# Results kept by lower and higher expert, with the last expert's second layer in another layout

## The reference

```python
S = Bb * Tt; C = int(CAP_FACTOR * S / E)                # 320 slots for each of 8 experts
probs = jax.nn.softmax(xf @ gate_w + gate_b, axis=1)
topk_p, topk_i = jax.lax.top_k(probs, TOP_K)            # two experts a token
topk_pn = topk_p / jnp.sum(topk_p, axis=1, keepdims=True)
...
xin = x_pad[idx]                                        # the rows of each expert's slots
h = jax.nn.relu(jnp.einsum('ecd,edh->ech', xin, w1) + b1[:, None, :])
out = jnp.einsum('ech,ehd->ecd', h, w2) + b2[:, None, :]
out = out * jnp.where(valid, tok_w, 0.0)[:, :, None]
final = jnp.zeros((S + 1, d), xf.dtype).at[idx.reshape(-1)].add(out.reshape(-1, d))[:S]
...
x = _layernorm(x + final, axis=-1)
```

## Time and profile before

| | us |
|---|---|
| runs, median (lowest to highest) | 478.04 (474.75 to 478.34) |
| profiled execution, its own time | 475.74 |
| its span, first to last instruction | 473.9 |
| busy: TensorE / VectorE / ScalarE / GpSimd | 402.7 / 363.5 / 243.4 / 145.9 |
| mean granted TensorE clock | 0.921 of full speed |

### The profile page before, as it was taken

The page is one execution under the profiler, slowest core; times in us unless marked ns, Lnnn a source line. Parts: engine busy times, 40 slices in busy tenths (PEclk is TensorE's granted clock), DMA queues, the critical chain, the costliest instruction groups (busy, mean ns, idle before and its releaser), DMA issues.

```text
span 473.9 us, 13604 instructions
## 1 busy us (share of the span) xinstructions
PE 402.7 (85%) x4701; PEld 306.7 (65%) x4701; DVE 363.5 (77%) x1553; ACT 243.4 (51%) x789; POOL 145.9 (31%) x240
## 2 busy tenths in 40 slices
PE   7999999999999999999997761699999999996000
PEld 4556776887888888888885661356776777674000
DVE  5678998888888888888886358867977898793284
ACT  1452666334343343443433253539888988861053
POOL 0056354223031120312203010241354345323384
PEclk9999999999999999999997685599999999999555
DMA  8769400201102011110200001064466545000582
GB/s 278 226 205 409 164 1 3 69 3 34 55 23 66 0 40 48 33 55 0 78 4 24 1 3 45 18 216 129 113 228 205 181 136 178 29 30 28 184 275 97
DMA packets 38238, 46.36 MB, mean 98 GB/s; under 512 B 4155, under 2 KB 32702, under 8 KB 38202
## 3 DMA queue, kind: packets, MB, share of 16 engines
q1 hardware_dynamic: 34474, 35.80, 23.4%
q0 software_dynamic: 3200, 9.40, 5.9%
q10 hardware_dynamic: 528, 0.69, 0.5%
HBM read 34.91 MB, written 11.01 MB: 97 GB/s over the span
## 4 chain that ended last, share of the span: by engine, by line
PE 60%; DVE 14%; ACT 8%; issue 8%; DMA 4%; POOL 3%; SPq 0%; ACTq 0%; POOLq 0%; DVEq 0%
PE bank L876 59%; ACT arena L788 3%; DMA wbuf<-in_w 2%; ACT arena L779 2%; DMA wbuf<-ybuf 1%; DVE kp L1743 1%; DVE vp L1723 1%; DMA bz<-in_b_rows 1%; ACT arena L818 1%; POOL rs L606 1%; PE bank L1252 1%; DVE ub L1331 1%; ACT kp L788 1%; DVE h L1342 1%; DVE mb L1333 1%
## 5 line engine op out<-in xcount | busy, mean ns | idle before, releaser
L623 ACT ACTIVATE rzb<-bank 128x32 f32<-128x32 f32 x128 | 25.4, 199 | 93.3 <-PE bank L876 93.2
L876 PE MATMUL bank<-h,whp 128*128 128x32 f16 x1143 | 59.2, 183 | 0.4 <-DVE h L1345 0.4
L876 PE MATMUL bank<-arena 128*128 128x320 f16 x384 | 54.6, 299 | 0.5 <-DVE arena L1770 0.5
L876 PE MATMUL bank<-arena,kp 128*128 128x320 f16 x384 | 54.5, 299 | 0.0
L1331 DVE TENSOR_TENSOR_SCAN ub<-rzb,bank 128x32 f32<-128x32 f32 x128 | 27.8, 218 | 28.9 <-ACT rzb L623 26.8
L626 ACT ACTIVATE nb<-ub 128x16 f32<-128x16 f32 x128 | 27.9, 218 | 42.2 <-DVE ub L1331 42.2
L876 PEld LDWEIGHTS bank<-arena 128*128 128x128 f16 x384 | 37.2, 99 | 15.0 <-DVE arena L1770 1.0
L876 PEld LDWEIGHTS bank<-arena,kp 128*128 128x128 f16 x384 | 37.3, 98 | 14.1
L876 PEld LDWEIGHTS bank<-h,whp 128*128 128x128 f16 x1143 | 40.8, 96 | 8.3 <-DVE h L1345 0.6
L876 PEld LDWEIGHTS bank<-hsb,at_w 66*64 66x64 f32 x256 | 25.1, 135 | 27.1 <-DVE hsb L1337 14.6
L577 POOL DMA_INDIRECT ybuf<-arena,six x24 | 24.1, 1006 | 59.3 <-DVE arena L1785 54.5
(11 more groups left out here) (214 smaller groups left out, 947.1 us busy)
## 6 DMA issues: line engine op xcount, KB each, us to landing
wbuf<-in_w SPq DMA_DIRECT2D x16, 1024.0 KB
ybuf<-zero POOLq DMA_DIRECT2D x8, 512.0 KB, 7.7
wbuf<-ybuf SPq DMA_DIRECT2D x16, 256.0 KB, 5.9
xin_t<-in_xT SPq DMA_DIRECT2D x16, 128.0 KB, 2.3
arena<-in_ctxT SPq DMA_DIRECT2D x4, 512.0 KB, 7.6
xfin_t<-in_xT SPq DMA_DIRECT2D x16, 128.0 KB, 2.2
xres<-in_xtok SPq DMA_DIRECT2D x16, 128.0 KB, 2.1
x_d<-x SPq DMA_DIRECT2D x8, 256.0 KB, 2.4
```

What stands on the lines that cost most here:

```text
L623: nc.scalar.activation(od(rzb[:]), RZ[j][:, s * 2 * B:(s + 1) * 2 * B], ACT.Sigmoid).then_inc(q["r_ready"], 1)
L876: return nc.tensor.matmul(out_, lhsT, rhs, start=start, stop=stop, skip_group_check=True)
```

## The change

Each token's two experts are sorted by number. The lower expert's result goes to row t of `ybuf`, the higher one's to row 2048 + t. `topf` gets the minimum and the maximum of the two numbers, and the weights `wt` are swapped to match, by twelve small operations that now stand behind expert 7's hidden layer on VectorE. The lower expert is never expert 7, so the lower half of `ybuf` is complete when expert 6 has been scattered. It is loaded as a whole (`ylow`, four DMAs of 512 KB, to the half of `wbuf` that expert 6's weights held) and added to x2 by VectorE, 16 operations. The higher half (`yhigh`, eight DMAs of 256 KB) follows when expert 7's rows have landed. The multiplications by ScalarE (line 857) and the additions by GpSimd (line 599) are gone.

To have expert 6 scattered early, its transposes move from the second layer of expert 7 to behind the third slice of its first layer, and its copies with them. The copies of expert 5 move ahead of the last two weight splits for expert 7.

The second layer of expert 7 is computed with the slots as rows (`rows_out`): the hidden rows are the stationary operand, the weights move, 3 blocks x 8 slices x 3 products = 72 matmuls of 256 columns. VectorE scales them and adds a row of bias (`b2r`, one more small load) and writes `yt` directly; each block is scattered as it becomes ready.

The semaphores `ctx_load0` to `ctx_load3` are renamed `quarter0` to `quarter3` and count the low loads too. Allocations, the further arguments and declarations are left out here.

```diff
+        ylow, yhigh = (view(wbuf, j * TILES * D, TILES, D) for j in range(2))
...
+            sp.dma_start(b2r[:], b2_last.to_broadcast([P, D])).then_inc(q["b2_row"], 16)
...
+            y_v = ybuf.rearrange("(j k p) d -> p j k d", j=2, p=P)
+            sp.wait_ge(q["w_lo"], 4 * (E - 1))
             for j in range(2):
-                sp.wait_ge(q[f"yst{j}"], 16 * CT * (E // 2))
-            y_v = ybuf.rearrange("(j k p) d -> p j k d", j=2, p=P)
+                sp.wait_ge(q[f"yst{j}"], 16 * CT * (E // 2 - j))
+            for i in range(4):
+                sp.dma_start(ylow[:, 4 * i:4 * i + 4, :], y_v[:, 0, 4 * i:4 * i + 4, :]).then_inc(q[f"quarter{i}"], 16)
+            sp.wait_ge(q["w_lo"], 4 * E)
+            sp.wait_ge(q["yst1"], 16 * CT * (E // 2))
             for c in range(CHUNKS):
-                for j in range(2):
-                    sp.dma_start(yg[c][:, 2 * j:2 * j + 2, :], y_v[:, j, 2 * c:2 * c + 2, :]).then_inc(q[f"yl{c}"], 16)
+                sp.dma_start(yhigh[:, 2 * c:2 * c + 2, :], y_v[:, 1, 2 * c:2 * c + 2, :]).then_inc(q[f"yl{c}"], 16)
...
-            scatter(E - 1)
-
-
-            def first_choice(c):
-                pool.wait_ge(q["c_w"], c + 1)
-                if c >= 2:
-                    pool.wait_ge(q["c_b"], 2 * c - 3)
-                pool.tensor_tensor(ca[2 * c % 4], yg[c][:, 0, :], x2[:, 2 * c, :], ALU.add).then_inc(q["c_even"], 1)
+
+            for c, m, col in slots(E - 1):
+                pool.wait_ge(q["yt_ready"], 2 * (E - 1) + c + 1)
+                pool.indirect_dma_start(
+                    ybuf[:, :], bass.IndirectOffsetOnAxis(ap=six[0:m, col], axis=0), yt[1][0:m, c, :], None,
...
-            first_choice(0)
             for c in range(CHUNKS):
-                if c + 1 < CHUNKS:
-                    first_choice(c + 1)
                 rstd_3(c)
 
...
+                if last:
+                    return
...
-            def weighted(c):
-                act.wait_ge(q[f"yl{c}"], 32)
-                nc.scalar.activation(yg[c][:, 0, :], yg[c][:, 0, :], ACT.Copy, scale=wt[:, 0, 2 * c:2 * c + 1]).then_inc(q["c_w"], 1)
-
-            weighted(0)
-            weighted(1)
             for c in range(CHUNKS):
-                if c + 2 < CHUNKS:
-                    weighted(c + 2)
                 act.wait_ge(q["rstd3"], c + 1)
...
+            def rows_out(e, j):
+
+                for c in range(CT):
+                    m = min(P, CAP - c * P)
+                    if c == 2:
+                        pe.wait_ge(q["yt_ready"], 2 * e)
+                    for f in range(FK):
+                        if c == 0:
+                            pe.wait_ge(q["h_lo"], FK * e + f + 1)
+                            if f % 4 == 0:
+                                pe.wait_ge(q["w_lo"], 4 * e + f // 4 + 3)
+                        for n, (a, b) in enumerate(PAIRS):
+                            last = mm(bank[(6, 7, 0)[c]][0:m, 0:D], hp[b][:, f, c * P:c * P + m], w2p[j][a][:, f, :],
+                                      f == n == 0, f == FK - 1 and n == 2)
+                    last.then_inc(q["last_mm"], 1)
+
...
+                    if f == 2 and last_:
+                        pe.wait_ge(q["yT_ready"], 2 * e)
+                        pe.wait_ge(q["yt_ready"], 2 * e - 2)
...
+                if last_:
+                    return rows_out(e, j)
...
                     if f == 3 and not first:
-                        if not last_:
-                            pe.wait_ge(q["xlo_ready"], 2 * e + 4)
-                        else:
-                            pe.wait_ge(q["yt_ready"], 2 * e - 2)
+                        pe.wait_ge(q["xlo_ready"], 2 * e + 4)
...
-            pe.wait_ge(q["yt_ready"], 2 * E - 2)
-            results_T(E - 1)
...
-            then(nc.vector.tensor_copy(topf[:], topi[:, :, 0:2]))
+            nc.vector.tensor_tensor(topf[:, :, 0], topi[:, :, 0], topi[:, :, 1], ALU.min)
+            then(nc.vector.tensor_tensor(topf[:, :, 1], topi[:, :, 0], topi[:, :, 1], ALU.max))
...
-            nc.vector.tensor_tensor(wsum[:], top[:, :, 0], top[:, :, 1], ALU.add).then_inc(q["ws_ready"], 1)
-            dve.wait_ge(q["ws_ready"], 1)
-            nc.vector.reciprocal(wsum[:], wsum[:]).then_inc(q["ws_ready"], 1)
-            dve.wait_ge(q["ws_ready"], 2)
-            for j in range(2):
-                nc.vector.tensor_tensor(wt[:, j, :], top[:, :, j], wsum[:], ALU.mult)
...
+                    if f == 2 and last:
+                        results(e - 1, 1 - j, 16 * CT * i)
...
-                    if p == 3 and not (isinstance(e, int) and e == 0):
+                    if p == (1 if isinstance(e, int) and e == E - 2 else 3) and not (last or isinstance(e, int) and e == 0):
...
-            results(E - 1, 1, 16 * CT * (E // 2 - 1))
-
+
+            ws = [0]
+
+            def weigh(ins):
+                ws[0] += 1
+                ins.then_inc(q["ws_ready"], 1)
+                dve.wait_ge(q["ws_ready"], ws[0])
+
+            nc.vector.tensor_tensor(turned[:], topi[:, :, 0], topi[:, :, 1], ALU.is_gt)
+            weigh(nc.vector.tensor_tensor(wsum[:], top[:, :, 0], top[:, :, 1], ALU.add))
+            nc.vector.tensor_scalar(kept[:], turned[:], -1.0, 1.0, ALU.mult, ALU.add)
+            weigh(nc.vector.reciprocal(wsum[:], wsum[:]))
+            for j in range(2):
+                nc.vector.tensor_tensor(wa[:, j, :], top[:, :, j], kept[:], ALU.mult)
+                last = nc.vector.tensor_tensor(wb[:, j, :], top[:, :, 1 - j], turned[:], ALU.mult)
+            weigh(last)
+            for j in range(2):
+                last = nc.vector.tensor_tensor(wa[:, j, :], wa[:, j, :], wb[:, j, :], ALU.add)
+            weigh(last)
+            for j in range(2):
+                last = nc.vector.tensor_tensor(wt[:, j, :], wa[:, j, :], wsum[:], ALU.mult)
+            weigh(last)
+
+            dve.wait_ge(q["b2_row"], 16)
+            dve.wait_ge(q["yst1"], 16 * CT * (E // 2 - 1))
+            for c in range(CT):
+                m = min(P, CAP - c * P)
+                dve.wait_ge(q["last_mm"], c + 1)
+                nc.vector.scalar_tensor_tensor(yt[1][0:m, c, :], bank[(6, 7, 0)[c]][0:m, 0:D], wund[1][0:m, 0:1], b2r[0:m, :],
+                                               ALU.mult, ALU.add).then_inc(q["yt_ready"], 1)
+
+
+            for k in range(TILES):
+                if k % 4 == 0:
+                    dve.wait_ge(q[f"quarter{k // 4}"], 16 + 16)
+                nc.vector.scalar_tensor_tensor(x2[:, k, :], ylow[:, k, :], wt[:, 0, k:k + 1], x2[:, k, :], ALU.mult, ALU.add).then_inc(q["c_low"], 1)
 
             for c in range(CHUNKS):
-                dve.wait_ge(q[f"yl{c}"], 32)
-                k = 2 * c + 1
-                nc.vector.scalar_tensor_tensor(ca[k % 4], yg[c][:, 1, :], wt[:, 0, k:k + 1], x2[:, k, :], ALU.mult, ALU.add).then_inc(q["c_odd"], 1)
+                dve.wait_ge(q[f"yl{c}"], 16)
+                dve.wait_ge(q["c_low"], 2 * c + 2)
+                if c >= 2:
+                    dve.wait_ge(q["o_ready"], c - 1)
                 for i in range(2):
                     k = 2 * c + i
-                    dve.wait_ge(q["c_odd" if i else "c_even"], c + 1)
-                    if c >= 2:
-                        dve.wait_ge(q["o_ready"], c - 1)
-                    nc.vector.scalar_tensor_tensor(cb[k % 4], yg[c][:, 2 + i, :], wt[:, 1, k:k + 1], ca[k % 4], ALU.mult, ALU.add).then_inc(q["c_b"], 1)
+                    nc.vector.scalar_tensor_tensor(cb[k % 4], yhigh[:, k, :], wt[:, 1, k:k + 1], x2[:, k, :], ALU.mult, ALU.add).then_inc(q["c_b"], 1)
                 for i in range(2):
                     k = 2 * c + i
                     dve.wait_ge(q["c_b"], k + 1)
```

22 lines of the change are left out of this document (14 added, 8 removed).

## The result

The changed kernel took 473.52 us in the median of 20 runs (471.34 to 477.25), the kernel before 475.82 beside it (20 runs, 473.57 to 478.42). The ratio is 0.9959, with a 95% interval from 0.9939 to 0.9979: about 1.9 us faster, where the prediction said 7.6. By its own bound of 1% that is no change. The sign held, and so did the stated range of 466 to 475; the size was forecast four times too large. That the range held is in part luck: it was laid around 470 from a median of 478.04 for the kernel before, and in these 20 runs that kernel took 475.82. From that level the forecast would have been 468.2.

The account below looks back on a forecast made before the run. The prediction took serial latency, engines waiting for one transfer or neighbour, as the bound at the end. Its terms, +0.1 - 5.2 - 2.5 = -7.6 us, gave 468.1 from the profiled execution, 470.4 on the median's level; it gave 470, range 466 to 475.

Parts of the forecast that it names:

- They bring nothing: Before expert 0: four small weight operations leaving VectorE's queue gain nothing, since TensorE multiplies filler until 312.12.
- a cost elsewhere: Anywhere else in the kernel: a cost that cancels the gain; chance 0.04.
- The landing of the last scatter: End of expert 7: SP issues the first high load 2.20 us after the last scatter's start, at 438.4.
- Rival 1: End of expert 7: low loads still flow, the last scatter lands 2 us later; -5.6, 472.4 us; chance 0.10.
- the 5.2 forecast: Start of the final chunks' sums after expert 7: at 442.0 instead of 447.19, -5.2 us.
- The ring: Final eight chunks of sums and norm: a pair takes 4.75 us (4.58 to 4.89), 20.5 for 22.98 in all, -2.5.
- Routing: Routing stage near 291 us: one cast becomes min and max, +0.1 us (bounds 0 and 0.2).
- Expert 5's results: Before expert 7: copies of 1.1 us move ahead of VectorE's last two weight splits; nothing is lost.
- Rival 2: Expert 7's second layer: columns don't count, 0.136 us a matmul; -5.7, 472.3 us; chance 0.10.
- Rival 4: Low loads: rows just written load slowly, at 100 GB/s +5.0, 483.0 us; chance 0.04.
- Rival 5: Final chunks: the pace stays 4.89 us a pair and only the start moves; -7.1; within the forecast's 0.64.
- Rival 3: End of expert 7: VectorE's sixteen adds lock out the last scatter's descriptors; -2.2, 475.8 us; chance 0.08.

Follow-up runs that it names:

- after_again: The changed kernel once more, unedited, for a second profile, timed beside the kernel before: 473.6 us, ratio 0.9969.
- the old layout: The changed kernel with the last expert's second layer, transposes, copies and three scatters as before the change: 481.53 us, ratio 1.0115.

## Why the prediction was off

**The step that failed: "They bring nothing: the tensor engine multiplies filler until 312.12".** It asked what the removed operations free, not what they hold back. Without them VectorE's first split starts 0.88 us after the first gather (306.02 and 305.14), where it was 1.59 (306.23 and 304.64), and this shift puts the second and third gather under the splits. TensorE then waits for rows, and in all profiles of this stretch but the first it multiplies at half its clock for a few us behind the wait. The cost is 1.4 us in the first profile (116.02 for 114.65) and 2.6 to 3.1 in the seven others; it is 3.1 in the ratios. The prediction had even named the sign of such a case ("the forecast is wrong if the stretch before 415 us changes by more than the 0.1") and gave a cost elsewhere only 0.04.

**The landing of the last scatter: "SP 2.20 after the last scatter's start".** It measured 3.94, and 4.63 in after_again. The 2.20 was read where no load was in flight. Rival 1 is this step, and its price (2 us later) was about right: 1.7 and 2.4. The prediction's own numbers held the collision: it had the low loads in by 438.0 to 440.7 and the last scatter start at 436.2 (435.4 + 0.77), so "in by 440.7 at the latest" was no argument against it. The data then needed 2.69 for 3.41, which gave 0.7 back. Two smaller terms went the same way. A matmul of 256 columns took 8.14 / 72 = 0.113 for 0.109, 0.29 us in all. The low loads went out at T + 11.43 for T + 10.6, so nearer to the last scatter: 0.6 of that because the scatters of expert 6 stand 1.66 and 1.52 apart instead of 1.28 (the first two end 0.86 and 0.85 us after the end of a split of hidden rows on VectorE), 0.2 because the last of them landed in 2.42. The ring started at T + 23.24 and 23.96 for T + 22.17: 1.1 to 1.8 us of the 5.2 forecast.

**The ring: "a pair takes 4.58 to 4.89, I take 4.75".** It took 5.01, outside the bounds: 1.83 of VectorE, 1.97 to ScalarE, 1.09, 0.12 back. The 1.88 taken as the disturbed step had one of GpSimd's operations beside an add (0.38 in the earlier trace rows); now the next chunk's adds come 0.16 us after the variance and meet two of them, 0.34 and 0.44 for 0.19 each. Cost: 0.86 us over the ring (21.36 for 20.5).

Together, with the usual 2.6 to 3.1 for the first step: -7.6 + (2.6 to 3.1) + (1.1 to 1.8) + 0.9 = -3.0 to -1.8, and -1.9 was measured (-2.9 to -1.0). With the old weight operations kept the first step is gone, and -7.6 + (1.1 to 1.8) + 0.9 = -5.6 to -4.9 stands against a measured -5.1.

**What was right.** Routing cost 0.1 (two operations at 291.49 and 291.60). Expert 6's rows were ready at T + 5.06, as worked out (T + 5.1). VectorE finished expert 7's last block at 437.00 = T + 15.84 for T + 15.6; the twelve weight operations took 1.7 us for 2.2 and delayed no block but the first. Sixteen adds took 6.40 (0.40 each). From ScalarE's end to the span's end it stayed 3.74. "Expert 5's results: nothing is lost" is right in its sum, as the run with them put back shows, though a scatter grew by 1.5 us.

**The rivals.** Rival 1 happened. Rival 2 (columns don't count) fell: 0.113, not 0.136. Rival 4 fell: the low half flowed at 352 GB/s. Rival 5, a ring that stays at 4.89, was too mild: it took 5.01 (and its sum is -7.2, not -7.1). Rival 3, the lock, fell at the place where it was looked for (1.22 us, not the whole run of adds) and was true at three others: the gathers of expert 0, expert 5's scatter (2.50), and the old layout (6.42). The prediction weighed it with a scatter beside VectorE operations of 0.3 to 0.5 us, where the loss of a turn is small: 1.04 there, and 1.35 and 1.21 beside the same operations in the changed kernel.

The Trainium skill, "SBUF — State Buffer", states in its part on the two sides of the memory that the pair of ports is an exclusive lock for a whole instruction. For VectorE operations with two SBUF inputs it adds that this holds only against a GpSimd operation that reads SBUF, a condition which the prediction left out. In its warning on DMAs issued from GpSimd's queue it says that GpSimd can't write the descriptors (the orders to the DMA engines) while VectorE runs an operation in a 2-port mode, as a float32 copy. These traces agree that GpSimd waits: each lengthened DMA ends 0.83 to 0.96 us after the end of a VectorE instruction, here one with two tensor inputs. That the one who starts first keeps the ports, as the page says, they show only for the VectorE instruction in progress: at its end the waiting DMA got its turn in some runs, and in the old layout it lost to adds that started after it. In the other direction they show no lock: a gather that started 0.13 us ahead of three splits (306.10 and 306.23, before) left them at 3.71 us, and the sixteen adds took 6.41 beside the long scatter and 6.42 alone.
